# Causal scores in 32x64 tiles, the convolution's own tap on ScalarE, and new orders of work in a four-stage decoder stack

## The reference, cut to what matters

```
conv = conv_b + sum(padded[:, k:k + L, :] * conv_w[:, k] for k in range(4))   # k = 3 is the token's own tap
energy = jnp.einsum('bhsk,bhtk->bhst', Q, K)                                  # attention 2, 16 heads of 16
energy = jnp.where(cols[None, :] > cols[:, None], -jnp.inf, energy)           # causal
scores = jnp.einsum('bqhd,bkhd->bhqk', Q_, K_) / D_HEAD ** 0.5                # attention 4
scores = jnp.where(causal, scores, jnp.float32(-1000000000.0))
```

## Time and profile before

| | us |
|---|---|
| median of 3 runs (1672.55 to 1675.62) | 1673.29 |
| the profiled execution's own time | 1675.6 |
| its span in the trace | 1673.8 |
| TensorE matmul busy | 1616.5 (97%) |
| TensorE weight load busy | 1393.2 (83%) |
| VectorE busy | 1387.1 (83%) |
| ScalarE busy | 1039.8 (62%) |
| GpSimd busy | 493.3 (29%) |

### The profile page before, as it was taken

The page is one execution under the profiler, slowest core; times in us unless marked ns, Lnnn a source line. Parts: engine busy times, 40 slices in busy tenths (PEclk is TensorE's granted clock), DMA queues, the critical chain, the costliest instruction groups (busy, mean ns, idle before and its releaser), DMA issues.

```text
span 1673.8 us, 61139 instructions
## 1 busy us (share of the span) xinstructions
PE 1616.5 (97%) x25060; PEld 1393.2 (83%) x25060; DVE 1387.1 (83%) x3585; ACT 1039.8 (62%) x2667; POOL 493.3 (29%) x1256
## 2 busy tenths in 40 slices
PE   7899999999999999999999999999999999999986
PEld 6777888888888888888888888888888888888774
DVE  4689888888888889888888988888898888898652
ACT  2355666766666676666667666666766666676652
POOL 2333223333322332332233233223323322333110
PEclk9999999999999999999999999999999999999997
DMA  6110000000000000000000000000000000000000
GB/s 216 52 64 21 6 18 31 18 25 28 22 3 24 25 24 24 25 17 9 24 25 25 25 24 22 5 24 25 24 25 24 17 10 24 21 28 19 5 5 7
DMA packets 31316, 44.37 MB, mean 27 GB/s; under 512 B 3008, under 2 KB 26176, under 8 KB 30912
## 3 DMA queue, kind: packets, MB, share of 16 engines
q1 hardware_dynamic: 31040, 40.45, 7.4%
HBM read 36.12 MB, written 4.33 MB: 24 GB/s over the span
## 4 chain that ended last, share of the span: by engine, by line
PE 55%; DVE 36%; issue 5%; POOL 2%; DMA 1%; ACT 1%; SPq 0%; DVEq 0%; POOLq 0%; ACTq 0%
PE ring L639 18%; PE ring L645 14%; PE ring L627 6%; DVE conv L1358 5%; DVE maxima_at L1258 5%; PE score L707 4%; DVE decay L1392 4%; PE score L731 3%; PE ring L773 3%; DVE decay L1396 2%; PE ring L858 2%; DVE conv L1364 2%; DVE QB L1269 2%; DVE conv L1353 2%; PE score L671 2%
## 5 line engine op out<-in xcount | busy, mean ns | idle before, releaser
L1533 POOL TENSOR_TENSOR stat<-stat 128x1 f32<-128x1 f32 x224 | 131.7, 594 | 617.2 <-DVE stat L1224 616.6
L1019 ACT COPY actT<-ring 128x256 f32<-128x256 f32 x256 | 95.5, 373 | 291.7 <-PE ring L627 290.5
L1258 DVE TENSOR_REDUCE maxima_at<-score 128x4 f32<-128x512 f32 x388 | 240.8, 684 | 25.5 <-PE score L707 24.5
L1052 ACT ACTIVATE weights<-score 128x512 f32<-128x512 f32 x388 | 200.7, 607 | 28.5 <-PE score L731 27.9
L1358 DVE SCALAR_TENSOR_TENSOR conv<-raw,vectors,conv 128x128 f32<-128x128 f32 x576 | 169.0, 349 | 6.8
L639 PE MATMUL ring<-actT,w_q 128*128 128x128 f32 x1024 | 141.5, 281 | 0.7 <-ACT actT L1019 0.7
L639 PEld LDWEIGHTS ring<-actT,w_q 128*128 128x128 f32 x1024 | 124.5, 191 | 12.8 <-issue 11.3
L639 PE MATMUL ring<-actT,w_up 128*128 128x128 f32 x1024 | 129.6, 281 | 0.5 <-ACT actT L1019 0.5
L639 PEld LDWEIGHTS ring<-actT,w_up 128*128 128x128 f32 x1024 | 121.1, 194 | 3.7 <-ACT actT L1019 1.1
L1184 ACT ACTIVATE gT<-ring,vectors 128x128 f32<-128x128 f32 x256 | 73.0, 368 | 72.2 <-PE ring L639 71.5
L645 PE MATMUL ring<-w_down,gT 128*128 128x256 f32 x512 | 115.9, 379 | 1.3 <-issue 1.3
(11 more groups left out here) (179 smaller groups left out, 3814.8 us busy)
## 6 DMA issues: line engine op xcount, KB each, us to landing
decay<-rates_out SPq DMA_DIRECT2D x32, 512.0 KB, 3.9
cT<-in_ctxT SPq DMA_DIRECT2D x32, 128.0 KB, 2.2
x_in<-in_x SPq DMA_DIRECT2D x32, 128.0 KB, 2.4
out<-result SPq DMA_DIRECT2D x32, 128.0 KB, 2.1
row_all<-in_rows SPq DMA_DIRECT2D x1, 1420.0 KB, 9.9
w_in<-in_in_proj SPq DMA_DIRECT2D x1, 1288.0 KB, 7.2
w_k<-in_k SPq DMA_DIRECT2D x4, 256.0 KB, 5.8
w_v<-in_v SPq DMA_DIRECT2D x4, 256.0 KB, 5.7
```

The costliest lines, as they stand in the source:

```text
L1019: nc.scalar.copy(dst.rearrange("p c k -> p (c k)"), t[:, 0:n]).then_inc(read, 1)
L1052: run(weights[:, turned_buffer(it, a_, l), r, :], score[:, r, :], ACT.Exp).then_inc(S["exps"], 1)
L1258: nc.vector.tensor_reduce(maxima_at[:, maxima_buffer(it, a_, l), :, 32 * r:32 * r + 17:16], score[:, r, :].rearrange("p (c f k) -> p c f k ...
L1533: tt(stat[:, l, 10:11], stat[:, l, 2:3], stat[:, l, 4:5], ALU.pow).then_inc(S[done], 1)
```

## The change

1. **Causal scores.** `causal_quads` and `causal_quadsT` replace `quads` and `quadsT` for attentions 2 and 4. Each of the 16 calls becomes two (j = 0, 1), with a tile of 32 rows by 64 columns. Of the two, one moves 64 columns and one 128; the quarter masked whole is not computed. For odd heads (e = 1) the halves are exchanged: queries (in `quadsT`: keys) 64 to 127 land on partitions 0 to 63. The mask laid first is exchanged likewise, with as many instructions as before.
2. **What the exchange asks for.** V of attentions 2 and 4 comes from `project_turned`: odd heads use the activations shifted by 64 tokens (`actT` and `cT` get 64 more columns, the DMA of the context brings 192 instead of 128), 4 calls of 128 columns instead of 2 of 256. `x2T` on ScalarE has a second copy of 64 columns by 2. `shifted` on VectorE has three instructions instead of two. Length masks compare with an exchanged index.
3. **Convolution.** After its copy to `raw`, `xbc` on ScalarE computes the own tap from PSUM, 3 activations for each half, and only then frees the ring bank. VectorE's L1353 instructions go, and with them one of the three waits between steps.
4. **Space.** `gT` has one buffer instead of two (`down` of an element must stand before `up0` of the next), `pad_u8` moves into another tensor, and the masks come in two DMAs of 384 KB instead of one of 512 KB.
5. **Orders.** All tables are new, and the filler calls go from 113 to 101.

The diff, cut to its core:

```diff
+            def project_turned(it, what, lane, w, xT):
+                t, full = claim(it, what, lane)
+                for e in range(2):
+                    for c in range(DC):
+                        last = mm(t[:, e * P:(e + 1) * P], xT[:, c, e * HALF:e * HALF + P], w[:, c, e * P:(e + 1) * P],
+                                  start=(c == 0), stop=(c == DC - 1))
+                last.then_inc(full, 1)
...
+            def causal_quads(it, a_, l):
+                evacuated_all(it, (f"Q{a_}", l), (f"K{a_}", l))
+                lay_causal(it, "quads", a_, l, 0)
+                for c in range(DC):
+                    for f in range(2):
+                        e, at = 1 - f, (2 * c + f) * P
+                        for r, rows_of in enumerate(ROWS_OF):
+                            keys = K2[rows_of, l, c, :] if a_ == 2 else KE[rows_of, l, c, e, :]
+                            for j in range(2):
+                                first, upto = HALF * (j ^ e), HALF * (j ^ e) + HALF
+                                last = mm(score[HALF * j:HALF * (j + 1), r, at:at + upto], QB[rows_of, l, c, e, first:upto], keys[:, 0:upto],
+                                          start=False, stop=(c == DC - 1 and f == 1))
+                                if c == DC - 1 and f == 1:
+                                    last.then_inc(S[f"scores{r}"], 1)
...
+            def causal_quadsT(it, a_, l):
...
+                            for j in range(2):
+                                first = HALF * (j ^ e)
+                                last = mm(score[HALF * j:HALF * (j + 1), r, at + first:at + P], KE[rows_of, l, c, e, first:first + HALF],
+                                          QB[rows_of, l, c, e, first:], start=False, stop=(c == DC - 1 and e == 1))
...
             def V_2(it, l):
                 evacuated(it, "x2T", l, ("V2", l))
-                project(it, "V2", l, square["v2"], actT[:, l])
+                project_turned(it, "V2", l, square["v2"], actT[:, l])
...
                 nc.scalar.copy(raw[:, l % 2, half * n:(half + 1) * n, TAPS - 1:],
-                               t[:, 0:n * P].rearrange("p (c k) -> p c k", c=n)).then_inc(read, 1)
+                               t[:, 0:n * P].rearrange("p (c k) -> p c k", c=n))
+                for k in range(n):
+                    c = half * n + k
+                    last = run(conv[:, l % 2, c, :], t[:, k * P:(k + 1) * P], ACT.Identity,
+                               scale=conv_w[:, c, TAPS - 1:TAPS], bias=conv_b[:, c:c + 1])
+                last.then_inc(read, 1)
...
-                for e in range(2):
-                    last = stt(QB[:, l, :, e, :], t[:, 0:D].rearrange("p (c k) -> p c k", c=DC), spare_row[:, e:e + 1],
-                               QB[:, l, :, e, :], ALU.mult, ALU.add)
+                parts = [(0, 0, 0, P), (1, 0, HALF, HALF), (1, HALF, 0, HALF)] if a_ in CAUSAL else [(0, 0, 0, P), (1, 0, 0, P)]
+                for e, to, at, n in parts:
+                    last = stt(QB[:, l, :, e, to:to + n], turned_max[:, :, at:at + n], spare_row[:, e:e + 1],
+                               QB[:, l, :, e, to:to + n], ALU.mult, ALU.add)
...
                     evacuated(it, f"xbc{half}", l)
-                    for c in chunks:
-                        last = ts(conv[:, l % 2, c, :], raw[:, l % 2, c, TAPS - 1:], conv_w[:, c, TAPS - 1:TAPS],
-                                  conv_b[:, c:c + 1], ALU.mult, ALU.add)
                     for k in range(TAPS - 1):
-                        step(last)
+                        if k:
+                            step(last)
```

More of the change, by code:

```diff
@@ L1 @@
+import itertools
 from contextlib import ExitStack
@@ L50 @@
 TASKS = dict(
[L51 to L58, removed]
@@ new lines @@
+    mT3=50.3947, mT4=60.6732, n2=42.2277, n3=49.4664, norm2=10.6565, norm3=88.4196, norm4=64.5188, norm5=71.7121, pairs=23.039,
+    proj=28.4681, quads1=31.2933, quads2=39.4747, quads3=47.8053, quads4=58.3005, quadsT2=41.3266, quadsT3=50.8474,
+    quadsT4=63.2348, row=45.3931, scan=22.9444, scores1=31.0852, scores2=-16.4311, scores3=-120.4105, scores4=143.0582,
+    silu=16.1007, softplus=16.4642, spread=27.4473, store=1.1553, turn1=33.8619, uT=27.1621, up0=67.8152, up1=68.5372,
+    values1=34.8732, values2=43.0989, values3=51.6754, values4=64.7774, x1=23.4405, x1r=14.414, x2T=36.8931, x3T=45.132,
@@ L194 @@
[L194 to L203 removed]
+        K2=3.0002, K4=1.8259, KE2=-23.8364, KE3=-17.929, Q1=2.7366, Q2=2.8538, Q3=3.805, Q4=3.3363, V1=1.019, V2=2.5581, V3=2.7065,
@@ new lines @@
+        Y=3.0684, attT2=-70.4472, attT3=59.1964, attT4=21.3918, ctxT=0.9059, exps2=79.7406, exps3=126.9152, exps4=19.9947,
+        fc1=2.7042, ld=2.946, row=2.6348, scores1=4.1533, silu=7.3535, softplus=5.858, turn1=2.4157, uT=2.5066, up0=2.4099,
+        up1=2.9829, x1=-6.8266, x2T=3.1118, x3T=2.8749, x4T=1.4027, x5T=2.1996, x6T=1.3886, xbc0=2.5283, xbc1=3.7761, xhatT=2.6997,
+        xnT=2.6155, z0=1.2777, z1=4.3482, K0=-19.217, Q0=-81.6684, V0=-23.7557, attT0=-4.9347, exps0=51.3358, prep_in=5.7522),
@@ L270 @@
 MAXIMA_AT, EXPS_AT = counted(SCORED), counted(EXPED)
+SCORED_BY = dict(zip(UNITS, itertools.accumulate(2 if unit[1] in CAUSAL else 1 for unit in UNITS)))
 class Of:
@@ L1090, in copied, with x2T @@
             def copied(what, n=D):
-                return lambda it, l: copy_out(it, what, l, actT[:, l], n)
+                return lambda it, l: copy_out(it, what, l, actT[:, l, :, 0:P], n)
+            def x2T(it, l):
+                t, read = filled(it, "x2T", l)
+                x2 = t[:, 0:D].rearrange("p (c k) -> p c k", c=DC)
+                nc.scalar.copy(actT[:, l, :, 0:P], x2)
+                nc.scalar.copy(actT[:, l, :, P:], x2[:, :, 0:HALF]).then_inc(read, 1)
             def V_1(it, l):
@@ L1144, in V_2 @@
             def V_2(it, l):
-                values_out(it, "V2", l, V2, H16, DH16)
+                t, read = filled(it, "V2", l)
+                run(V2[:, l, :, 0:DH16].rearrange("p (j e) d -> p e j d", e=2), t[:, 0:D].rearrange("p (e j d) -> p e j d", e=2, d=DH16),
+                    ACT.Copy).then_inc(read, 1)
             def row(it, l):
```

412 lines of the change are left out of this document (215 added, 197 removed).

## The result

The change made the kernel slower by about 1%: 1690.45 us median (1682.33 to 1695.68, 4 runs) against 1672.92 (1671.79 to 1675.62), a ratio of 1.0098 with a 95% interval of [1.0056, 1.014]. The forecast was 1648 in 1632 to 1675. The profiled execution took 1695.7 us, its span 1693.9.

What follows compares the result with a forecast made beforehand. TensorE's instruction list, 97% busy, was taken as the bound. The terms -26.4 - 6.2 + 1.3 + 4.8 - 2 + 3 = -25.5 us took the profiled 1675.6 to 1650, as median 1648, range 1632 to 1675.

Steps and rivals of the forecast that it cites:

- Scores: Causal units on TensorE: half tiles in independent queues cut a unit from 1.10 to 0.88 us, 26.4 us gained.
- in step: Rival on the causal scores: unequal tiles wait for each other, so no gain there; 1674 us, chance 0.11.
- Handed out at Y's pace: Rival on the causal scores: 64 matmuls come 16 ns each, 1.03 us a unit; 1666 us, chance 0.07.
- Order: TensorE's task sequence: 24 changes of shape between tasks instead of 26, 0.10 us each, 6.2 us less in all.
- V: V products on TensorE: eight matmuls of 128 columns instead of four of 256, 0.02 us each, 1.3 us more.
- Maxima: VectorE's maxima: 0.15 us more a unit, paid between mT2 and quadsT2, 4.8 us more; waits behind QB to about 12.
- Convolution and ring: Own tap moved to ScalarE: 2 us gained from TensorE's waits for VectorE, 3 us lost when ScalarE comes late.
- ScalarE holds the ring: Rival at z1 behind xbc0 and V3 behind xbc1: late ScalarE stalls TensorE every period; 1.1 us gives 1683; chance 0.08.
- Start and end: Start and end of the run: fewer fillers and more DMA cost nothing, 0 us with 4 either way.
- The signs of being wrong: Forecast wrong if the period changes by under 0.4 us or TensorE's busy share falls below 95% in the middle.

Runs made afterwards that it cites:

- e4: Changed kernel with every half tile moving 64 columns, leaving out needed scores, so not the reference's output: 1683.6 us (one run).
- e13: Changed kernel with one burst of 1024 more weight load and matmul pairs (32x32 bfloat16 tiles), no wait among them, put in once: 1718.7 us.
- e18: Changed kernel with four trains of 96 float32 weight load and matmul pairs, of differing weight widths and moved columns, put in once: 1703.7 us.
- e5: Changed kernel with 96 more TensorE instructions, put in once before the steady periods by laying one mask four times: 1689.8 us (one run).
- e6: Changed kernel with attention 4's transposed unit in whole tiles, 64 instructions fewer there, not the reference's output: 1671.14 us, ratio 0.9994.
- e8: Kernel before with the convolution's own tap on ScalarE, V2 and V4 in eight products and the edits of space: 1684.88 us, ratio 1.0075.
- e1: Changed kernel with causal scores in whole 32x128 tiles again, new orders and ScalarE's own tap kept: 1679.86 us, ratio 1.0056.
- e7: Changed kernel with V1 moved between values1 and attention 4's transposed unit, and ScalarE's copy of V1 moved ahead too: 1716.58 us, ratio 1.0259.
- e14: Changed kernel with one task's 16 matmuls moved ahead of V3's four wide ones, burst 288 instructions instead of 320: 1696.2 us, ratio 1.0138.
- e9: Changed kernel with whole tiles, no exchange, V2 and V4 in four products, all taps on VectorE, leaving the new orders alone: 1713.72 us.
- B of e18: The train of 96 float32 pairs with 32x32 weights and 64 moved columns, in the changed kernel with four trains put in: 1703.7 us.
- e3: Changed kernel with V1 moved on TensorE between values1 and quadsT4, ScalarE's copy left where it was: 1793.3 us, ratio 1.0738.
- e17: Changed kernel with attention 1's values in 128x128 weights, 16 pairs in place of 64: 1715.4 us, ratio 1.0263.

## Why the prediction was wrong

The profiled execution was forecast at 1650.1 us and took 1695.7: 45.6 us. Undisturbed periods account for 28 x (0.82 - 0.43) = 11 us, the irregular time for 26, start and end for 8 (5.6 measured, and 2.5 forecast to be gained there).

- **Scores, the step that failed, first for its size.** The halves do run ahead of each other as independent queues; "in step" was wrong. The columns were priced rightly too, as e4 shows (0.21 us for 0.22). What failed is the rest of the unit. The sum had 0.16 us fixed and 0.05 for handing out, 0.21 in all; measured are 1.05 - 0.67 = 0.38 (e4: 0.85 - 8 x 0.057 = 0.39). I wrote "handing out all 64 needs 0.76, which is less", as if the handing out ran beside the columns for nothing. In the unit 32 pairs start in 0.35 us, one more follows, then a hole of 0.08 us, and the next seven calls come 16.6 ns apart (the two lines below, up to 454.80 and 454.88 us); e13 and e18 have the hole at the same place. That the hole and the pace behind it make up the whole 0.17 us is argued, not shown. "Handed out at Y's pace" had the number nearly right (1.03), but not the mechanism: e4 hands out the same 64 in 0.85. Gain 0.05 a unit, 5 to 6 us instead of 26.4.

```profile
L775 PE MATMUL score<-QB,KE x32: 214/266/318, 454.4 to 454.8; 32*64 32x128 f32 x16, 32*64 32x64 f32 x16
L775 PE MATMUL score<-QB,KE x33: 214/267/318, 454.4 to 454.8; 32*64 32x128 f32 x17, 32*64 32x64 f32 x16
```

- **Scores, what no step held.** 64 instructions more in each unit, one of them behind `e3` and `values1`: a burst of 320 instructions in 2.3 us against 258 in 2.5 before. I looked at columns and queues, and never at whether instructions arrive. 13 gaps, together 14 us in that unit, others behind it, and 10 us between 100 and 1550 us at 1.2 GHz. By e5 and e6 these stops follow the place and the length of the burst; that the instruction supply is what is late is the reading that fits them, and e13 shows such stops in a burst by itself.
- **Order.** Forecast -0.2 us a period; the new orders gave -0.66 with ScalarE's tap (e8 to e1), much of it by taking the ring wait away that the tap makes. Better than forecast.
- **V.** +0.02 to 0.03 us per V, as forecast.
- **Maxima.** The idle of the mask's loads behind `QB` went from 6.9 to 8.9 us, not to 12. The step was right, its size too large.
- **Convolution and ring.** "ScalarE holds the ring" is real in the old orders (0.35 us a period at `project_T`, e8), not in the new ones. VectorE was less free than I said: the pairs' wait for it is 8.0 us now, and the moves near it that I tried cost 0.7 to 1.5 us a period (e7, e14; e9, with all taps on it again, 1.5).
- **Start and end.** Forecast 0 with 4 either way; +5.6. Why isn't known.
- **The signs of being wrong.** I named two, a period changed by less than 0.4 us and a busy share below 95% in the middle. Neither came: 0.43 us, and 98% (196.34 of 200 us). Both look at the common period or the mean, and the loss sits in the odd periods.

The sign was lost by the second point: without the added irregular time the profiled execution would be some 6 us faster than before (12.0 less 5.6). e6 shows it from the other side: 64 instructions fewer brought 19 us.

## What to carry to other kernels

Count instructions as well as columns. When small tiles double the pairs of a stretch that is already dense, ask how many instructions run there in a row without a slow one: in the new orders, with some 220 of them ahead, a crossing of a block of 256 can stop TensorE for 0.3 to 2 us, and its clock may be halved afterwards. The edge isn't sharp: a burst of 258 never stopped the old kernel, one of 256 stopped e1 four times, one of 320 the changed kernel thirteen times. An average rate read from one short burst is no rate for a longer one, and in a full pipeline edits don't add: try each in the order it will run in.

## What the runs showed of the hardware that I had not expected

- TensorE starts some 32 pairs of narrow tiles at once (0.12 us for bfloat16 in e13, 0.21 for float32 in B of e18). Then comes a hole of 0.06 to 0.24 us, and behind it a pair comes in 8.3 to 8.7 ns at best, in both types and at 2.4 and at 1.2 GHz (e13, e18, the old `values1`).
- In an endless burst a block of 256 instructions takes 3.5 to 4.0 us, of which 2.2 to 2.8 is standing (e13, at 1.2 GHz); a crossing with a slow stretch ahead of it costs nothing (before: no gap over 0.33 us within an operation in the periods).
- After two of the four gaps of 1.7 to 2.0 us in the changed kernel's half unit the granted clock fell to 1.2 GHz (6.8 us in all); with e3's holes of 2.6 us it fell in most periods (92 us).
- Weights of 128x128 with 33 columns take 0.12 us a pair in float32 (e17), close to the 0.11 with 128 columns.
